# First expert's weights and rows fetched before the recurrence ends, receptance mix moved from the finish phase into the experts

## The chip, the cores and the metric

One core of one Trainium2 chip runs the whole program as one launch. The metric is the time of one execution on the device in microseconds (us), the median of the runs.

## What is computed

The input x has 16 sequences of 512 steps and 512 features; a conditioning vector per sequence goes in as well. Four blocks are chained as residuals:

```python
x = x + _L0_cond_ref(x, cond_1024[:, None, :], ...)   # 16-tap convolution, projections, decayed scan over time
x = x + _L1_cond_ref(x, cond_1024, Wx, Wh, b)          # an LSTM of 512 units over 512 steps
x = x + _L2_cond_ref(x, itok, cond_1024, ...)          # 16 experts, with a receptance gate
x = x + _L3_cond_ref(...)                              # a mask by thresholds along time, as abs(x) >= gathered
```

What the change touches is the third block (the fourth is listed for its place in the code):

```python
xprev = jnp.concatenate([shift_state[:, None, :], x[:, :-1]], axis=1)
dxprev = xprev - x
xk = x + dxprev * time_maa_k
xr = x + dxprev * time_maa_r
...
expert_in = buf[:E * C].reshape(E, C, D)
h = jnp.square(jax.nn.relu(jnp.einsum('ecd,edf->ecf', expert_in, w_key)))
expert_out = jnp.einsum('ecf,efd->ecd', h, w_value)
...
r = jax.nn.sigmoid(jnp.einsum('btd,ed->bte', xr, w_recept))
return r * y
```

Each token has an expert by a hash of its id, and a slot in this expert's buffer of 512 rows. The rows xk are scattered to these slots, the experts run, and their output rows are gathered back, multiplied by the receptance r and added.

## The kernel before

Three functions run one after another, each in a block of its own, with a program for each engine and a barrier of all engines at the end (`recur_phase`, block from line 203; `expert_phase`, from line 932; `finish_phase`, from line 1122). Order within an engine is written out by hand, with semaphores between engines. SP issues the plain loads and stores, POOL (GpSimd) the scatters, gathers and stores of expert outputs; ACT is ScalarE, DVE VectorE and PE TensorE. At the end of a block every engine drains, and the block's line carries these instructions.

`recur_phase` computes the first two blocks in 32 tiles of 16 time steps. PE multiplies the hidden state by Wh (line 415) and, between the steps, the next tile's inputs by Wx in three products of split operands (lines 888 to 890, `split_products`); DVE transposes, adds and makes the cell; ACT does the nonlinear functions. Ahead of the first tile stands a prologue: the 16-tap convolution of tiles 0 and 2 on DVE (`convolve`, lines 644 and 648), of tile 1 on PE with diagonal matrices (`convolve1`, line 372, four filters of 32 instructions), the outputs of the first block (`outputs`, lines 385 and 386), the sum `add_block` (line 701), and the split of its result into a high part on ACT (`split_high`, line 521) and a low part on DVE (`split_low`, line 715). PE's last work before the first step are `inputs(2, q)` (line 363) and `project(2, 0)` (line 351). `load_window` on SP (line 217) waits for a count of `u_part`, which `inputs` raises. Wh is loaded by ACT (line 586) once the four filters are evicted, since it takes the memory of the diagonal matrices; when it has landed, POOL fills the expert rows in memory with zeros (line 316, 16 stores of 1 MB).

For each tile, x2 (the residual after the LSTM) is stored to `x2_scratch` by SP, and twice a tile 128 rows xk are mixed (ACT line 539, DVE line 726), transposed by PE (line 396), copied by ACT (`keep_rows`, line 548) and scattered by POOL (line 309). There is one buffer `rows` and one `index`; both the copy and the index wait until the scatter before has landed. The last two scatters, after the last tile, close the phase.

`expert_phase` runs 16 experts of 512 rows. SP loads rows (line 939), wk (946) and wv (951), 1, 2 and 2 MB. PE transposes the rows of the next expert (973) in the middle of the first product, ACT and DVE split rows, wk and wv into high and low parts (ACT 1015 and 1032, DVE 1051 to 1059 and 1076). The first product takes 8 groups f of 12 matmuls, whose relu and square ACT makes (1027, 1031); the second takes 4 groups a of 24, evicted by ACT (1041) and stored by POOL (960). For expert 0, rows, wk and wv are first loaded after the barrier.

`finish_phase` takes the 16 sequences (batches) in turn. POOL gathers the rows of outputs (1154, four of 256 KB for a batch) and puts the first column of each x2 buffer in place (`halo`, 1159); SP loads x2 (1128). ACT weighs the previous step (`weigh_last`, 1231), DVE mixes it in (`mix_in`, 1297), PE multiplies by w_recept (`receptance`, 1194: 32 instructions for a batch, in two banks by turns), and ACT opens the gate from it (`open_gate`, 1239). PE transposes the gathered rows (`turn`, 1205) and DVE combines gate, rows and x2 (`combine`, 1308 and 1311). Then comes the mask: ACT takes absolutes with a sum (1246), DVE inverts it (`invert`, 1315 and 1319), ACT exponentiates (1254), DVE scans along time (1326), ACT takes the sides of a limit (1263), DVE chooses, searches (1341) and keeps (1350), POOL multiplies (1180) and SP stores (1139). In DVE's loop the order for batch i is:

```python
scan(i)
bound(i)
if i + 1 < B:
    combine(i + 1)
if i + 3 < B:
    mix_in(i + 3)
choose(i)
if i + 1 < B:
    invert(i + 1)
search(i)
keep(i)
```

## Time and profile before

| | us |
|---|---|
| Median of 3 runs (lowest, highest) | 4111.47 (4107.68, 4112.68) |
| The profiled execution | 4110.3 |
| Its span, first to last instruction | 4108.6 |
| PE busy | 3880.3 (94%) |
| DVE busy | 3022.5 (74%) |
| ACT busy | 1696.7 (41%) |
| POOL busy | 290.3 (7%) |

The mean granted clock of PE over the span was 0.985 of full speed. The span has three stages: the recurrence to about 2982 us, the experts from the first product at 3015.4 to the last at 3765.3, and the finish phase, whose first scan starts at 3815.6. Since the phases have different bounds, the shares above say little by themselves; busy times have to be read in windows, and the seams between phases in a timeline. A row of the timeline has the start, the duration, the engine, line and operation, what is written and read, the count, and in brackets how long the engine was idle before it and what ended that.

### The profile page before, as it was taken

To read this page: it belongs to the slowest core of one execution; us is meant where nothing else is said; L and a number is where in the kernel's file an instruction comes from. 1 tells how busy PE (TensorE), PEld (TensorE's weight loads), DVE (VectorE), ACT (ScalarE), POOL (GpSimd) and SP (SyncE) were. 2 spreads that over 40 slices of the span, in tenths; PEclk is the share of its full clock that TensorE was granted. 3 is DMA by queue.
4 is the path that set the end of the run, shared out by engine and by line. 5 is a ranking of instruction groups with operands and counts; after the bars stand their busy time and mean duration, and the time that the engine had idled before them with its cause. 6 is when DMAs were issued, how large, how long until landed. Compare 5 with 4: busy or idle time off the path is not lost. (4 is left out here: it accounts for less than half of the span.)

```text
span 4108.6 us, 111991 instructions
## 1 busy us (share of the span) xinstructions
PE 3880.3 (94%) x44162; PEld 2552.2 (62%) x44162; DVE 3022.5 (74%) x9889; ACT 1696.7 (41%) x5364; POOL 290.3 (7%) x362
## 2 busy tenths in 40 slices
PE   7999999999999999999999999999769999997995
PEld 6566666666656666665666666666457888775442
DVE  7888888888878888887888888875545544552798
ACT  5334333333433333343333333433234444443675
POOL 1000000000000000000000000000000000001343
PEclk9999999999999999999999999999989999998998
DMA  6311111112111111211111112100043343333353
GB/s 241 83 29 27 27 35 27 33 37 30 27 28 35 27 32 30 37 27 28 27 35 27 32 36 31 27 17 15 12 166 123 137 157 135 123 113 123 123 185 113
DMA packets 387868, 266.99 MB, mean 65 GB/s; under 512 B 288953, under 2 KB 322233, under 8 KB 384292
## 3 DMA queue, kind: packets, MB, share of 16 engines
q1 hardware_dynamic: 365648, 184.21, 18.1%
q0 software_dynamic: 17696, 66.79, 4.2%
q10 hardware_dynamic: 4020, 9.10, 0.6%
q8 instruction: 339, 5.55, 0.6%
q14 instruction: 165, 1.35, 0.1%
HBM read 176.48 MB, written 83.92 MB: 63 GB/s over the span
## 5 line engine op out<-in xcount | busy, mean ns | idle before, releaser
L415 PE MATMUL bank<-buf,buf 128*16 128x256 f32 x32768 | 1872.3, 380 | 64.3 <-DVE buf L754 55.0
L415 PEld LDWEIGHTS bank<-buf,buf 128*16 128x16 f32 x32768 | 905.9, 97 | 885.6 <-DVE buf L754 81.8
L888 PE MATMUL bank<-buf,buf 128*128 128x256 f32 (+1 forms) x3072 | 1036.0, 337 | 5.6 <-DVE buf L1059 2.7
L889 PE MATMUL bank<-buf,buf 128*128 128x256 f32 (+1 forms) x3072 | 977.7, 318 | 0.0
L890 PE MATMUL bank<-buf,buf 128*128 128x256 f32 (+1 forms) x3072 | 977.1, 318 | 0.0
L648 DVE SCALAR_TENSOR_TENSOR buf<-buf,buf,buf 128x256 f32<-128x256 f32 x1860 | 846.7, 481 | 0.8 <-issue 0.8
L732 DVE STREAM_TRANSPOSE buf<-bank 128x256 f32<-128x256 f32 x1024 | 459.6, 449 | 447.4 <-PE bank L415 407.8
L604 ACT ACTIVATE buf<-buf 128x96 f32<-128x96 f32 x1024 | 290.6, 284 | 1137.8 <-DVE buf L737 1137.5
L888 PEld LDWEIGHTS bank<-buf,buf 128*128 128x128 f32 x3072 | 580.7, 189 | 255.7 <-issue 216.2
L890 PEld LDWEIGHTS bank<-buf,buf 128*128 128x128 f32 x3072 | 582.8, 190 | 41.1
L889 PEld LDWEIGHTS bank<-buf,buf 128*128 128x128 f32 x3072 | 583.6, 190 | 38.6
L607 ACT ACTIVATE buf<-buf 128x32 f32<-128x32 f32 x1024 | 235.1, 230 | 631.1 <-DVE buf L749 631.1
L1071 DVE CAST buf<-buf 128x512 fp32r<-128x512 f32 x128 | 54.6, 427 | 355.6 <-ACT buf L1031 352.2
L737 DVE SCALAR_TENSOR_TENSOR buf<-buf,buf 128x128 f32<-128x128 f32 x1024 | 295.6, 289 | 21.1 <-DVE buf L732 1.4
L1194 PE MATMUL bank<-buf,buf 128*128 128x512 f32 x512 | 231.4, 607 | 46.6 <-DVE buf L1297 23.7
L309 POOL DMA_INDIRECT expert_in_scratch<-buf,buf x64 | 80.6, 1260 | 2414.1 <-ACT buf L548 2371.2
L527 ACT ACTIVATE buf<-bank,buf 128x256 f32<-128x256 f32 x512 | 233.9, 457 | 15.1 <-PE bank L890 15.1
L754 DVE SCALAR_TENSOR_TENSOR buf<-buf,buf 128x32 f32<-128x32 f32 x1024 | 193.8, 189 | 62.2 <-ACT buf L607 14.2
L749 DVE SCALAR_TENSOR_TENSOR buf<-buf,buf 128x32 f32<-128x32 f32 x1024 | 196.5, 192 | 36.0 <-DVE buf L746 0.7
L605 ACT ACTIVATE buf<-buf 128x32 f32<-128x32 f32 x1024 | 218.6, 213 | 0.0
L1194 PEld LDWEIGHTS bank<-buf,buf 128*128 128x128 f32 x512 | 97.0, 194 | 169.8 <-issue 136.2
L743 DVE SCALAR_TENSOR_TENSOR buf<-buf,buf 128x32 f32<-128x32 f32 x1024 | 176.5, 172 | 17.9 <-ACT buf L604 14.8
(143 smaller groups left out, 2969.2 us busy)
## 6 DMA issues: line engine op xcount, KB each, us to landing
buf<-in_wk SPq DMA_DIRECT2D x16, 2048.0 KB, 9.9
buf<-in_wv SPq DMA_DIRECT2D x16, 2048.0 KB, 9.3
buf<-in_xT SPq DMA_DIRECT2D x62, 496.0 KB, 3.9
buf<-in_xB SPq DMA_DIRECT2D x32, 512.0 KB, 3.8
expert_in_scratch<-buf POOLq DMA_DIRECT2D x16, 1024.0 KB, 22.2
x_scratch<-buf SPq DMA_DIRECT2D x32, 512.0 KB, 9.6
buf<-expert_in_scratch SPq DMA_DIRECT2D x16, 1024.0 KB, 11.9
expert_out_scratch<-buf POOLq DMA_DIRECT2D x64, 256.0 KB, 4.8
```

The source lines that it names most:

```text
L415: last = mm(gate_ps[hf][32 * j:32 * j + B, 0:HCOLS], hist[:, k, at_step(slot_at)], wh[:, k, j * GCOLS + hf * HCOLS:j * GCOLS + (hf + 1) * ...
L527: a(xw[par][:, :, q, :], xw_ps[q % 2][:, 0:LTILE].rearrange("p (b t) -> p t b", b=B), ACT.Identity, bias=bias[:, q:q + 1], scale=0.5).then ...
L604: a(gate[hf], pre[hf][:, 0:6, :], ACT.Tanh, scale=0.5).then_inc(s["ifo_ready"][hf], 1)
L605: a(gcand[hf], pre[hf][:, 6:8, :], ACT.Tanh).then_inc(s["g_ready"][hf], 1)
L607: a(tanh_c[hf], cell[hf], ACT.Tanh, scale=0.5).then_inc(s["tc_ready"][hf], 1)
L648: v.scalar_tensor_tensor(out=conv[:, k, :], in0=src, scalar=taps[:, k, i:i + 1], in1=conv[:, k, :], op0=ALU.mult, op1=ALU.add).then_inc(s[ ...
L732: v.transpose(turned_g[hf].rearrange("p g b -> p (g b)"), gate_ps[hf][:, 0:HCOLS])\
L737: v.scalar_tensor_tensor(out=pre[hf], in0=turned_g[hf][:, :, 0:B], scalar=0.5, in1=xw[par][:, st, 8 * hf:8 * hf + 8, :], op0=ALU.mult, op1 ...
L888: nc.tensor.matmul(out, left[0], right[0], start=first, stop=False)
L889: nc.tensor.matmul(out, left[0], right[1], start=False, stop=False)
L890: return nc.tensor.matmul(out, left[1], right[0], start=False, stop=last)
L1194: last = nc.tensor.matmul(r_ps[m % 2][:, 0:T], wr[:, k, m * P:(m + 1) * P], xr[i % 2][:, k, :], start=k == 0, stop=k == KD - 1)
```

## The change

It has six parts.

1. In the prologue the order changes on three engines. PE runs `project(0, 1)` and `inputs(0, 1)` ahead of the third filter, and the fourth filter behind `outputs(0, ...)` and `inputs(1, ...)`. ACT evicts the first two filters, splits x1, then evicts the other two and loads Wh. DVE runs `convolve(2, 1, ...)` ahead of `split_low(1, 1, ...)`.
2. SP loads wk and wv of expert 0 in the recurrence's last tile, into memory that the recurrence no longer uses; ACT and DVE split wk at the end of their programs of the recurrence.
3. The last scatter has a row buffer of its own and takes its index straight from `slot`; so neither the copy nor the scatter waits for the scatter before.
4. SP loads the rows of expert 0 in the recurrence's block, when all scatters have landed.
5. Weighing and mixing for the receptance leave the finish phase. In each expert e, SP loads x2 of batch e with its first column (`load_x2`, the column as a copy from a small buffer `halo` in fast memory), ACT weighs one of four parts after each eviction of y, DVE mixes the parts after the split of the next wk, and SP stores the result to a new scratch `xr_scratch`, once the mix is complete. This wait, store and load stand in SP's program ahead of the loads of the next expert's wk.
6. The finish phase loads the mixed rows (`load_mixed`, three buffers). w_recept, the first three mixed rows and x2 of batches 0 and 1 are loaded during the last expert, and PE and ACT run the receptance and gate of batches 0 and 1 at the end of the experts' block.

```diff
--- before.py
+++ after.py
@@ -111,6 +116,7 @@
     window = carve(KD, WIN)
     center = carve(KD, LTILE)
     conv = carve(KD, LTILE)
+    rows_last = carve(D, at=carve.top)
     x1_hi, x1_lo = ([carve(KD, LTILE, dt=F32R) for _ in range(2)] for _ in range(2))
...
@@ -255,10 +261,17 @@
                     load_window(n + 4, 1)
 
             tiles(sp, tile)
+            sp.wait_ge(s["xw_summed"], NBLK * NLT)
+            first.load_wk(sp, ins, 0)
+            sp.wait_ge(s["pre_ready"][0], LSTEPS * (NLT - 1))
+            sp.wait_ge(s["pre_ready"][1], LSTEPS * (NLT - 1))
+            first.load_wv(sp, ins, 0)
             sp.wait_ge(s["x2_done"], 2 * NLT)
             sp.dma_start(x2_d.rearrange("p c b t -> p (c b) t")[:, :, (NLT - 1) * LSTEPS:],
                          stream[3].rearrange("p c b t -> p (c b) t")[:, :, 1:])\
                 .then_inc(s["x2_stored"][1], 16)
+            sp.wait_ge(s["scattered"], 16 * 2 * NLT)
+            first.load_rows(sp, rows_d, 0, 0)
             for par in range(2):
                 sp.wait_ge(s["x2_stored"][par], 16 * NLT // 2)
...
@@ -318,6 +331,14 @@
             pool.dma_start(y_d[E * CAP:E * CAP + 1, :], zeros[0:1, 0:D]).then_inc(s["zero_stored"], 16)
             g.tensor_scalar(stream[0][:, :, :, 0], cond, 2.0, None, ALU.mult).then_inc(s["halo_ready"], 1)
 
+            def scatter_last():
+                r = 2 * NLT - 1
+                pool.wait_ge(s["rows_ready"], r + 1)
+                pool.sem_inc(s["pool_passed"], 1)
+                g.indirect_dma_start(out=rows_d, out_offset=bass.IndirectOffsetOnAxis(ap=slot[:, r:r + 1], axis=0),
+                                     in_=rows_last, in_offset=None, bounds_check=E * CAP - 1,
+                                     oob_is_err=False).then_inc(s["scattered"], 16)
+
             def tile(n, pair, four, ahead):
                 if later(n, 1):
...
@@ -331,8 +352,8 @@
                         scatter(n - 1, u)
 
             tiles(pool, tile)
-            for u in range(2):
-                scatter(NLT - 1, u)
+            scatter(NLT - 1, 0)
+            scatter_last()
             pool.wait_ge(s["scattered"], 16 * 2 * NLT)
 
         @block.tensor
...
@@ -428,15 +449,15 @@
             project(0, 0)
             inputs(0, 0)
             convolve1(1)
-            convolve1(2)
             project(0, 1)
             inputs(0, 1)
-            convolve1(3)
+            convolve1(2)
             pe.wait_ge(s["steps"], 7)
             for q in range(2):
                 outputs(0, q)
             for q in range(2):
                 inputs(1, q)
+            convolve1(3)
             for q in range(2):
                 project(1, q)
...
@@ -543,6 +564,9 @@
             def keep_rows(m, u):
                 r = 2 * m + u
                 act.wait_ge(s["rows_turned"], r + 1)
+                if isinstance(r, int) and r == 2 * NLT - 1:
+                    a(rows_last, rows_ps[:, :], ACT.Copy).then_inc(s["rows_ready"], 1)
+                    return
                 if later(m, 1) or u:
                     act.wait_ge(s["scattered"], 16 * r)
...
@@ -580,12 +604,17 @@
             soft_last(0)
             state_high(0)
             act.wait_ge(s["proj_part"], 2)
-            for k in range(KD):
+            def keep_conv1(k):
                 act.wait_ge(s["conv1_summed"], k // 2 * 2 + 2)
                 a(conv[:, k, :], conv_ps[k], ACT.Identity, bias=conv_b[:, k:k + 1]).then_inc(s["conv1_ready"], 1)
-            act.dma_start(wh, ins["Wh"]).then_inc(s["wh_landed"], 16)
+
+            for k in range(2):
+                keep_conv1(k)
             for q in range(2):
                 split_high(0, 0, q)
+            for k in range(2, KD):
+                keep_conv1(k)
+            act.dma_start(wh, ins["Wh"]).then_inc(s["wh_landed"], 16)
             soft_first(1)
             soft_last(1)
...
@@ -624,6 +653,7 @@
             for u in range(2):
                 weigh_last(NLT - 1, 3, u)
                 keep_rows(NLT - 1, u)
+            first.high_wk(act, 0)
 
         @block.vector
...
@@ -840,9 +870,9 @@
                 state_part(1, i)
             for q in range(2):
                 add_block(1, 0, 1, q)
+            convolve(2, 1, 0, CONVS // 2)
             for q in range(2):
                 split_low(1, 1, q)
-            convolve(2, 1, 0, CONVS // 2)
 
             def tile(n, pair, four, ahead):
...
@@ -880,6 +910,7 @@
             tiles(dve, tile)
             for u in range(2):
                 mix_in(NLT - 1, 3, u)
+            first.low_wk(dve, 0)
 
 
...
+        sp.dma_start(self.wk_raw, ins["wk"][:, bass.ds(e * KD, KD), :]).then_inc(self.s["wk_landed"], 16)
+
+    def load_wv(self, sp, ins, e):
+
+        sp.dma_start(self.wv_raw, ins["wv"][:, bass.ds(e * KF, KF), :]).then_inc(self.s["wv_landed"], 16)
+
+    def load_rows(self, sp, rows_d, e, par):
+
+        src = rows_d[bass.ds(e * CAP, CAP), :].rearrange("(a p) d -> p a d", p=P)
+        sp.dma_start(self.rows[par], src).then_inc(self.landed[par], 16)
+
+    def high_wk(self, act, e):
+
+        act.wait_ge(self.s["wk_landed"], 16 * (e + 1))
+        for k in range(KD):
+            self.nc.scalar.activation(self.wk_hi[:, k, :], self.wk_raw[:, k, :], ACT.Copy)\
+                .then_inc(self.s["wk_hi_ready"], 1)
...
+class Gating:
+
+    RING, XR_RING = 6, 3
+
+    def __init__(self, nc, ctx, carve, banks):
+        self.nc = nc
+        self.stream = [carve(KD, T) for _ in range(self.RING)]
+        self.gate = [carve(KD, T) for _ in range(2)]
+        self.wr = carve(KD, D)
+        self.xr = [carve(KD, T) for _ in range(self.XR_RING)]
...
+    def load_mixed(self, sp, xr_d, i):
+
+        if i >= self.XR_RING:
+            sp.wait_ge(self.s["r_summed"], KD * (i - self.XR_RING + 1))
+        sp.dma_start(self.xr[i % self.XR_RING], xr_d[:, :, i, :]).then_inc(self.xr_landed[i % self.XR_RING], 16)
+
+    def receptance(self, pe, i):
+
+        pe.wait_ge(self.xr_landed[i % self.XR_RING], 16 * (i // self.XR_RING + 1))
+        for m in range(KD):
+            if i >= 1 or m >= 2:
+                pe.wait_ge(self.s["gate_ready"], KD * i + m - 1)
+            for k in range(KD):
+                last = self.nc.tensor.matmul(self.r_ps[m % 2][:, 0:T], self.wr[:, k, m * P:(m + 1) * P],
+                                             self.xr[i % self.XR_RING][:, k, :], start=k == 0, stop=k == KD - 1)
+            last.then_inc(self.s["r_summed"], 1)
...
-                    sp.wait_ge(s["wk_ready"], KD * e)
-                sp.dma_start(wk_raw, ins["wk"][:, bass.ds(e * KD, KD), :]).then_inc(s["wk_landed"], 16)
+                    sp.wait_ge(first.s["wk_ready"], KD * e)
+                    first.load_wk(sp, ins, e)
                 if not is_last(e):
                     load_rows(e + 1, 1 - par)
                 if later(e, 1):
                     sp.wait_ge(s["wv_ready"], KF * e)
-                sp.dma_start(wv_raw, ins["wv"][:, bass.ds(e * KF, KF), :]).then_inc(s["wv_landed"], 16)
+                    first.load_wv(sp, ins, e)
+                if later(e, 1):
+                    sp.wait_ge(s["xr_made"], KD * e)
+                    store_mixed(e - 1)
+                else:
+                    sp.dma_start(maa_r, ins["maa_r"]).then_inc(s["maa_landed"], 16)
+                    sp.wait_ge(s["halo_made"], 1)
+                load_x2(e)
 
             experts(sp, one)
+            sp.wait_ge(s["turned"], KD * E)
+            sp.wait_ge(first.s["wk_ready"], KD * E)
+            sp.wait_ge(s["xr_stored"], 16 * (E - 1))
+            sp.dma_start(gating.wr, ins["wr"]).then_inc(gating.s["wr_landed"], 16)
+            for i in range(gating.XR_RING):
+                gating.load_mixed(sp, xr_d, i)
+            sp.wait_ge(s["h_summed"], KF * E)
+            for i in range(2):
+                gating.load(sp, x2_d, i)
+            sp.wait_ge(s["xr_made"], KD * E)
+            store_mixed(E - 1)
+            sp.wait_ge(s["xr_stored"], 16 * E)
 
         @block.gpsimd
         def _(pool):
...
 
             experts(pe, one)
+            pe.wait_ge(s["xT_ready"], KD * E)
+            pe.wait_ge(gating.s["wr_landed"], 16)
+            for i in range(2):
+                gating.receptance(pe, i)
 
...
-                act.wait_ge(s["wk_landed"], 16 * (e + 1))
-                if later(e, 1):
-                    act.wait_ge(s["h_summed"], KF * e)
-                for k in range(KD):
-                    nc.scalar.activation(wk_hi[:, k, :], wk_raw[:, k, :], ACT.Copy).then_inc(s["wk_hi_ready"], 1)
-
-            split_wk(0)
+                act.wait_ge(s["h_summed"], KF * e)
+                first.high_wk(act, e)
+
+            def weigh_last(e, k):
+                if k == 0:
+                    if not later(e, 1):
+                        act.wait_ge(s["share_ready"], 2)
+                    act.wait_ge(s["x2_landed"], 32 * (e + 1))
+                    if later(e, 1):
+                        act.wait_ge(s["xr_stored"], 16 * e)
+                nc.scalar.activation(xr_row[:, k, :], x2_row[:, k, 0:T], ACT.Copy, scale=maa_last[:, k:k + 1])\
+                    .then_inc(s["weighed"], 1)
 
             def one(e, par):
-                act.wait_ge(s["wv_landed"], 16 * (e + 1))
+                act.wait_ge(first.s["wv_landed"], 16 * (e + 1))
                 if later(e, 1):
                     act.wait_ge(s["y_summed"], NS * e)
...
@@ -1039,8 +1201,11 @@
                     elif a >= 2:
                         act.wait_ge(stored[a % 2], 16 * (a // 2))
                     nc.scalar.activation(y[a % 2], y_ps[a % 2][:, :], ACT.Copy).then_inc(s["y_ready"], 1)
+                    weigh_last(e, a)
 
             experts(act, one)
+            for i in range(2):
+                gating.open_gate(act, i, 0, KD)
 
         @block.vector
...
                     if f > TURN_FROM and f <= TURN_FROM + KD and not is_last(e):
                         split_x(e + 1, 1 - par, f - TURN_FROM - 1)
                 if not is_last(e):
-                    split_wk(e + 1)
+                    first.low_wk(dve, e + 1)
+                for k in range(KD):
+                    mix_in(e, k)
 
...
+                gating.load(sp, x2_d, i)
+                if i + 1 < RING:
+                    gating.load_mixed(sp, xr_d, i + 1)
             for i in range(B):
-                sp.wait_ge(s["final_ready"], i + 1)
+                sp.wait_ge(final_ready, i + 1)
                 sp.dma_start(out.rearrange("p (k b t) -> p k b t", k=KD, b=B)[:, :, i, :], final).then_inc(stored, 16)
                 if i + RING < B:
-                    load(i + RING)
+                    gating.load(sp, x2_d, i + RING)
+                    gating.load_mixed(sp, xr_d, i + RING)
             sp.wait_ge(stored, 16 * B)
 
...
-                        pe.wait_ge(s["gated_ready"], KD * (i - 1) + k + 1)
+                        pe.wait_ge(gated_ready, KD * (i - 1) + k + 1)
                     for c in range(NC):
                         last = nc.tensor.transpose(t_ps[k][:, c * P:(c + 1) * P],
                                                    rows[i % 2][c][:, k * P:(k + 1) * P], ident)
                     last.then_inc(s["turned"], 1)
 
-            pe.wait_ge(s["weights_landed"], 16)
-            receptance(0)
             turn(0)
-            receptance(1)
             turn(1)
-            receptance(2)
+            gating.receptance(pe, 2)
             for i in range(B):
                 if i + 2 < B:
                     turn(i + 2)
...
```

## Rows read from the trace of the kernel before

**Rows 1.** Windows by stage: busy us (and count) by engine, granted clock, DMA share, GB/s.

```profile
3015.44:3765.25 749.81, 730.42 (x3312) 599.19 (x3312) 369.16 (x567) 318.81 (x509) 34.08 (x63) 1.00 0.35 128
3765.25:3815.55 50.30, 25.33 (x65) 11.69 (x64) 14.09 (x26) 14.13 (x28) 14.46 (x23) 0.76 0.59 212
3848.38:4086.52 238.14, 202.60 (x620) 99.12 (x618) 233.83 (x441) 172.81 (x436) 107.68 (x72) 0.97 0.45 159
```

**Rows 2.** Timelines of PE and of DVE in the prologue.

```profile
51.09 7.17 PE L372 MATMUL bank<-buf,buf 128*128 128x256 f32 x32
97.79 3.65 PE L415 MATMUL bank<-buf,buf 128*16 128x256 f32 x64
...
95.99 1.29 DVE L715 TENSOR_TENSOR buf<-buf,buf 128x512 fp32r<-128x512 f32 x2 [12.37 <-ACT buf L521]
97.85 11.96 DVE L648 SCALAR_TENSOR_TENSOR buf<-buf,buf,buf 128x256 f32<-128x256 f32 x30
```

**Rows 3.** Line 217, its load issued at 96.0: time from issue to landing.

```profile
DMA to landing us min/median/max: 11.1/11.1/11.1
```

**Rows 4.** Timeline of all engines at the end of the recurrence.

```profile
2987.03 1.09 PE L396 MATMUL bank<-buf,buf 128*128 128x128 f32 x4 [2.37 <-DVE buf L726]
2990.85 0.60 ACT L548 ACTIVATE buf<-bank 128x512 f32<-128x512 f32 x1 [4.36 <-DMA expert_in_scratch<-buf,buf]
...
2992.31 0.97 POOL L309 DMA_INDIRECT expert_in_scratch<-buf,buf  x1 [1.20 <-ACT buf L548]
```

**Rows 5.** Line 203, the recurrence's block: duration (ns) and start of POOL's drain.

```profile
L203 POOLq DRAIN  x1: 6692/6692/6692, 2995.3 to 2995.3; - x1
```

**Rows 6.** Timeline of PE and DVE at the first expert's start.

```profile
3007.58 1.97 PE L973 MATMUL bank<-buf,buf 128*128 128x128 f32 x8 [19.46 <-DMA buf<-expert_in_scratch]
...
3013.47 0.69 DVE L1053 TENSOR_TENSOR buf<-bank,buf 128x512 fp32r<-128x512 f32 x1
...
3015.44 0.77 PE L888 MATMUL bank<-buf,buf 128*128 128x512 f32 x1 [2.73 <-DVE buf L1059]
```

**Rows 7.** Timeline of ACT in expert 1: its first relu, its split of wk.

```profile
3067.52 0.60 ACT L1027 ACTIVATE buf<-bank 128x512 f32<-128x512 f32 x1 [2.26 <-PE bank L890]
...
3091.59 3.90 ACT L1015 ACTIVATE buf<-buf 128x1024 fp32r<-128x1024 f32 x4
```

**Rows 8.** Line 946, the 16 loads of wk: time from issue to landing.

```profile
DMA to landing us min/median/max: 9.1/9.9/10.5
```

**Rows 9.** Line 932, the experts' block: duration (ns) and start of POOL's drain.

```profile
L932 POOLq DRAIN  x1: 5279/5279/5279, 3768.9 to 3768.9; - x1
```

**Rows 10.** Timelines of POOL, PE and DVE at the start of the finish phase.

```profile
3779.04 0.95 POOL L1154 DMA_INDIRECT buf<-expert_out_scratch,buf  x1 [0.30 <-issue]
...
3789.15 16.56 PE L1194 MATMUL bank<-buf,buf 128*128 128x512 f32 x32 [23.75 <-DVE buf L1297]
...
3806.26 0.69 DVE L1308 SCALAR_TENSOR_TENSOR buf<-buf,bank 128x512 f32<-128x512 f32 x1 [10.63 <-PE bank L1205]
```

**Rows 11.** Line 1154, the 64 gathers: time from issue to landing.

```profile
DMA to landing us min/median/max: 3.7/6.9/8.2
```

**Rows 12.** Timelines of DVE and PE in the finish phase's periods.

```profile
3962.02 2.73 DVE L1297 SCALAR_TENSOR_TENSOR buf<-buf,buf,buf 128x512 f32<-128x512 f32 x4
...
4051.52 1.91 PE L1205 MATMUL bank<-buf,buf 128*128 128x128 f32 x16
4053.27 13.90 PE L1194 MATMUL bank<-buf,buf 128*128 128x512 f32 x32
4067.00 1.91 PE L1205 MATMUL bank<-buf,buf 128*128 128x128 f32 x16
...
4071.10 4.55 DVE L1326 TENSOR_TENSOR_SCAN buf<-buf,bank 128x512 f32<-128x512 f32 x4
4081.97 0.17 DVE L1315 TENSOR_SCALAR buf<-buf 128x4 f32<-128x4 f32 x1 [0.71 <-ACT buf L1246]
4086.52 4.55 DVE L1326 TENSOR_TENSOR_SCAN buf<-buf,bank 128x512 f32<-128x512 f32 x4
```

208 lines of the change are left out of this document (93 added, 115 removed).

## The prediction

> **What bounds the kernel now.** I read the busy table by stages first, then at each seam between stages the timeline of all engines, then the instructions of single lines. Three phases follow one another, each an instruction block with a barrier at its end. The recurrence (to about 2982 us) is a chain of small steps that the change doesn't touch. The experts are TensorE work: PE is busy 730.4 of 749.8 us [rows 1], so work added on ScalarE (ACT) or VectorE (DVE) there is free while it fits its gaps. In the finish phase DVE is busy 233.8 of 238.1 us from the second scan to the sixteenth, PE 202.6 [rows 1]: DVE bounds it. Between the last expert product (3765.25) and the second scan (3848.38) lie 83.1 us, with a granted clock of 0.76 up to the first scan (3815.55) [rows 1]: a fill whose chain is serial. The change works on the fill at three seams and on the finish period. Times below are those of the profile before, and a gain at an early seam is not carried into the times of a later one.
>
> **Prologue.** Before, DVE waited 12.37 us for ACT's split of x1 (L521) at 95.99, and only then did the 32 operations of the second half convolution, which end at 109.8; PE had begun the first recurrent products at 97.79 and was done by 101.4 [rows 2]. With the convolution ahead of the split, DVE runs it in that wait: from 83.6 for some 12.6 us, then the split, at about 97.9. What is late next is PE. Its fourth filter (7.17 us [rows 2]) now stands behind the outputs and inputs, so that the load of Wh issues some 6 us later, and the products I work out 0.6 us later; TensorE's first step would come at about 101 instead of 109.7, a gain of 8.5. But in this step DVE convolves with a window whose load PE's inputs release; it took 11.1 us from its issue at 96.0 [rows 3] and would land at 107.7, when that convolution could have begun at 103. It began at 111.9, 2.1 after the transpose; I take 111.9 - 107.7 = 4.2. Bounds: 8.5 if the window is early, -1 if the filter and the later Wh load cost more and the landing takes 16 us beside the zero stores, which shift too.
>
> **From the recurrence to the first expert's products.** Before, the last rows' copy on ACT waited 4.36 us for the scatter ahead of it, and began at 2990.85 though PE's transposes were done at 2988.1 [rows 4]. With a buffer of its own it runs at 2988.15 to 2988.75; GpSimd (POOL) needed 0.86 us from the copy's end to the scatter [rows 4], so the scatter issues at 2989.6 in place of 2992.31. Before, POOL's drain began 3.0 after the issue and took 6.69 us, to 3002.0, which opened the next block [rows 5]. The first scatter may now overlap, so I allow 0.2: the barrier opens at 2999.5, 2.5 earlier (the bounds are 0, if the drain waits for the same last packet, and 3). The rows' load is released by the scatters, about 2992.5, and is there by 2998; weights come in the last tile, whose ACT and DVE waits are long. So PE transposes at 2999.8 instead of 3007.58 (it had waited 19.46 for the rows), DVE's split of x needs 6.58 (3007.58 to 3014.16), and the first product, which waited 2.73 more for the weights' split, starts at 3006.4 instead of 3015.44 [rows 6]. ACT's and DVE's splits of wk (four each, 3.9 us on ACT [rows 7]) lie under the drain, ended by 2995. Gain 9.0. Bounds: 6 with a later drain, 11 if the clock comes back sooner.
>
> **Experts.** Added to each: four ACTIVATEs, four DVE operations of 2.73 us together (those of L1297 [rows 12]), a 1 MB load, a 1 MB store and a load of 512 single elements. ACT's last one stands between the last eviction and the next expert's relu, where ACT sat idle 2.26 us [rows 7]; it needs 0.62. DVE's then ends before the relu is squared. On SP's queue the new wait for the mixed row stands ahead of the next wk load, and moves it from 3052 to about 3068.5. It is needed at 3091.59 [rows 7], and such a load takes 9.1 to 10.5 us [rows 8]; with 2 MB ahead of it I allow 16, against 23. The next rows' load, behind it, has an expert's length to spare. Cost 0; bounds 0 and +0.5 per expert, 8 in all, for a queue that I can't see.
>
> **The seam to the finish phase.** Before: the drain of POOL ended at 3774.2 [rows 9], eight gathers were issued with the fourth at 3779.04, the halo operations stood behind them, the first receptance ran 3789.15 to 3805.7 (16.56 us for 32 instructions, which take 13.90 at full clock [rows 10, 12]), and DVE's first combine began at 3806.26 [rows 10]. Now receptances 0 and 1 follow the last expert product without a barrier, still at full clock: 3765.25 + 2 x 13.75 = 3792.8. Their inputs were loaded from 3731 on. The barrier now waits for PE and ACT, not for the drain: 3793.6, 19.4 later than before. The fourth gather issues 4.84 after it, at 3798.4, and lands 6.9 later (median of 64, range 3.7 to 8.2 [rows 11]): 3805.3. The transposes, on a cold PE, let combine begin at 3806.5, so nothing is won up to there. Without the mixing behind it the chain from combine to scan is 1.86 shorter (next part): the first scan is at 3813.9 instead of 3815.55 [rows 1], gain 1.6, bounds -1 and +5. From there before took 32.8 us to the second scan [rows 1], since receptance 1 and 2 stood before its combine. Now combine 1 runs at once; receptance 2 starts about 3812.2 cold, its second quarter ends near 3821.6 (a quarter is 3.4 us, and I add 2.7 for the cold clock, as 16.56 against 13.90), then nine ACTIVATEs of 512 columns (gate, four sides, four absolutes), about 0.65 each by the 0.60 of [rows 7] and so 5.9 as an estimate, and DVE's rest of 4.55 (4081.97 to 4086.52 [rows 12]): second scan at 3832.2, 18.3 after the first. Gain 14.5, bounds 12 and 17.
>
> **The finish period.** DVE loses 2.73 us of mixing per batch [rows 12], but not all comes back. At the end, where no batch is left to mix, the scans start 15.42 apart (4071.10, 4086.52), and DVE waits 0.71 us for ACT's last absolute [rows 12]: mixing had covered that. Before, 12 periods lasted (238.14 - 2 x 15.42) / 12 = 17.27 [rows 1]. PE is next: transposes and receptance start 1.75 apart, the receptance takes 13.90 with 0.16 of it under its neighbour [rows 12], together 15.49. I take PE's 15.49. Coupling: ACT opens two gates at once after its exponents; with the mixing's ACTIVATEs gone it does so 2.5 us earlier, and I estimate a slack of about 1 us for PE's phase against DVE's in which neither side waits (gate 0 is out some 3.7 after a scan's start, and gate 1 may be out as late as 5.4 before ACT's sides delay the absolutes). Twelve periods of 17.27 become 15.49 and the last two stay within 0.1: 21.3. Bounds: 8 if each handshake costs 1.1 us more, 22.
>
> **Sum.** 4.2 + 9.0 + 0 + 1.6 + 14.5 + 21.3 = 50.6. The profiled execution took 4110.3 (span 4108.6, 1.7 around it), 1.2 less than the median of 4111.47. Forecast: 4110.3 - 50.6 = 4059.7, say 4060. Its own range is 4052 to 4068.
>
> **Rivals.** *Handshakes on PE.* When PE and DVE both need 15.4 to 15.5 us, waits for gates add up instead of hiding. For it: PE waited for ACT's gate in each period before. Against it: the gate follows earlier. With 1.1 us in each of 13 periods, 4074. Chance 0.14.
>
> *Gathers late.* SP queues five loads of 1 MB at the moment of the first gathers. If the gathers shared so badly that they took twice their median, 13.8 us, combine would begin 6.9 later, and the time is 4067. Against it: none of 64 gathers took over 8.2 [rows 11], beside loads that were issued with them. Chance 0.06. The Trainium skill, DMA: Bandwidth & Descriptors, "Issuing engines are not separate DMA queues", says that DMAs of all issuing engines run on the same 16 engines and interleave. By that rule POOL's gathers do share with SP's loads, which speaks for this rival; the landings bear out a sharing, not a place at the end.
>
> *The early parts don't bite.* If the drain ends when it did and the window's load holds the prologue, the two seams give 6.5 rather than 13.2, and the time is 4067, at the rim of my range; with one more shortfall, 4072. Chance 0.06.
>
> *More than forecast.* The window lands early and the gathers in 4 us: 4060 - 4 - 4 = 4052, down to 4047. Chance 0.06.
>
> *Slower than before.* The wk load of the next expert, held behind the wait for the mixed row, lands after ACT needs it; ACT's queue then holds the evictions of y behind it, and PE stalls. It decides from a landing of 23 us, and from 27 (3.6 us x 14 experts = 50) the kernel is slower. At 30 us: 4060 + 7 x 14 = 4158. Landings of 9.1 to 10.5 [rows 8] speak against it. Chance 0.02, and 0.02 for a landing near 26, which would eat the gain: 4060 + 3 x 14 = 4102.
>
> **How the numbers follow.** Forecast within its own range 0.64; the rest above. The range for 8 in 10 takes in the forecast's range and most of the cases next to it: 4050 to 4076. A measurement can tell about 0.2%, 8 us. Faster by more: 0.96; within it: 0.02 (the landing near 26); slower by more: 0.02.
>
> **What would show it.** First recurrent transpose near 101, the convolution behind it near 108; first expert product 9 us earlier; 47.0 us per expert as before; receptances straight behind the last product at 13.75 each; scans 15.5 apart, with PE almost gapless. Wrong would be: ACT waiting for wk, PE stalls behind the evictions, scans 16.5 or more apart, a combine that starts after 3812.

## The result, and the profile after

The changed kernel takes 4068.86 us (median of 4 runs, 4065.98 to 4069.88) against 4111.86 for the kernel before (4107.68 to 4112.68): a ratio of 0.9896, 95% interval 0.9879 to 0.9913. That is 43.0 us less where 50.6 were forecast, and 8.9 us over the forecast of 4060. The profiled execution took 4065.98 us with a span of 4064.0, which is 44.6 less than the span before.

Windows by stage of the changed kernel, from the first expert product to the last eviction of y, from there to the first scan, and from the second scan to the sixteenth; columns as in [rows 1], whose windows have the same cuts but for 3765.25, which lies 0.19 ahead of the last eviction (3765.44):

```profile
3001.55:3760.66 759.11, 739.75 (x3313) 600.53 (x3314) 412.00 (x629) 357.58 (x571) 34.13 (x63) 1.00 0.49 175
3760.66:3809.00 48.34, 35.05 (x102) 17.86 (x101) 6.54 (x12) 9.79 (x21) 12.79 (x17) 0.86 0.47 173
3824.50:4041.57 217.07, 199.22 (x620) 100.05 (x618) 203.86 (x393) 146.19 (x388) 110.05 (x62) 0.96 0.65 229
```

The first row is the surprise. The experts take 9 us longer than before, and PE is busy 9.3 us longer (739.75 against 730.42, 0.2 of it already the first receptance) on the same products at the same granted clock. The third row is the forecast gain of the finish. By stage, as differences of the same events in the two traces:

| stretch | before | after | forecast gain | measured gain |
|---|---|---|---|---|
| start to the last but one copy of rows (prologue) | 2984.70 | 2980.19 | 4.2 | 4.5 |
| from there to the first expert product | 30.74 | 21.36 | 9.0 | 9.4 |
| first product to last eviction of y (experts) | 750.00 | 759.11 | 0 | -9.1 |
| last eviction to first scan | 50.11 | 48.34 | 1.6 | 1.8 |
| first to second scan | 32.83 | 15.50 | 14.5 | 17.3 |
| second to sixteenth scan | 238.14 | 217.07 | 21.3 | 21.1 |
| sixteenth scan to the end | 22.1 | 22.4 | 0 | -0.3 |
| sum | | | 50.6 | 44.6 |

**Prologue.** DVE's timeline, which answers to [rows 2] and [rows 3]:

```profile
83.54 11.96 DVE L678 SCALAR_TENSOR_TENSOR buf<-buf,buf,buf 128x256 f32<-128x256 f32 x30
95.43 1.27 DVE L745 TENSOR_TENSOR buf<-buf,buf 128x512 fp32r<-128x512 f32 x2
99.29 0.45 DVE L762 STREAM_TRANSPOSE buf<-bank 128x256 f32<-128x256 f32 x1 [2.58 <-PE bank L436]
...
106.68 0.41 DVE L674 TENSOR_SCALAR buf<-buf,buf,buf 128x256 f32<-128x256 f32 x1 [5.17 <-DMA buf<-in_xT]
```

The convolution fills the old wait, the first transpose comes 10.4 us earlier, and then DVE waits 5.17 us for the window's load, as the forecast said it would (it expected 101 and 108; the rows say 99.3 and 106.7).

**To the first product.** Timeline of ACT, POOL and PE at the end of the recurrence, and the row of POOL's drain (line 209), which answer to [rows 4 to 6]:

```profile
2983.64 0.60 ACT L568 ACTIVATE buf<-bank 128x512 f32<-128x512 f32 x1 [1.65 <-PE bank L417]
...
2985.11 0.98 POOL L338 DMA_INDIRECT expert_in_scratch<-buf,buf  x1 [2.48 <-ACT buf L568]
...
2994.95 1.94 PE L1126 MATMUL bank<-buf,buf 128*128 128x128 f32 x8 [11.35 <-PEq L209]
...
3001.55 0.79 PE L919 MATMUL bank<-buf,buf 128*128 128x512 f32 x1 [1.51 <-DVE buf L1218]
```

```profile
L209 POOLq DRAIN  x1: 6692/6692/6692, 2988.0 to 2988.0; - x1
```

The last copy no longer waits for the scatter ahead of it. The drain has the same 6692 ns, and PE now waits for the block (L209) and not for the rows. PE's transposes and DVE's split of x are what is left between the barrier and the first product.

**Seam to the finish.** Timeline of PE, POOL and DVE; it answers to [rows 10, 12]:

```profile
3760.46 27.63 PE L1006 MATMUL bank<-buf,buf 128*128 128x512 f32 x64
...
3793.63 0.94 POOL L1309 DMA_INDIRECT buf<-expert_out_scratch,buf  x1 [0.30 <-issue]
...
3800.20 3.64 PE L1340 MATMUL bank<-buf,buf 128*128 128x128 f32 x16 [12.11 <-DMA buf<-expert_out_scratch,buf]
3801.43 0.69 DVE L1409 SCALAR_TENSOR_TENSOR buf<-buf,bank 128x512 f32<-128x512 f32 x1 [12.20 <-PE bank L1340]
...
3805.02 1.94 PE L1340 MATMUL bank<-buf,buf 128*128 128x128 f32 x16 [1.18 <-DMA buf<-expert_out_scratch,buf]
3806.80 13.90 PE L1006 MATMUL bank<-buf,buf 128*128 128x512 f32 x32
```

Two receptances take 27.63 us straight behind the last product, and PE then waits 12.11 us for the gathers. From line 1309, the 64 gathers, the answer to [rows 11]:

```profile
DMA to landing us min/median/max: 3.7/6.8/8.6
```

These are all 64 gathers of the phase. At the seam itself five loads of SP's queue, 1 MB each, were issued from 3788.99 on, and the fourth gather, issued at 3793.63, had landed when the transposes began at 3800.20: at most 6.6 us. So the gathers landed as before.

### The profile page after: what moved, and what is told of

Same layout as the page of the kernel before. It is cut to its first block and busy times, and to the rows that moved or that the text cites. A ratio compares the mean times of both kernels' runs of the same rounds, so it can differ in the third digit from the quotient of the medians.

```text
span 4064.0 us, 112079 instructions
## 1 busy us (share of the span) xinstructions
PE 3882.5 (96%) x44162; PEld 2553.4 (63%) x44162; DVE 3026.2 (74%) x9889; ACT 1700.8 (42%) x5364; POOL 302.9 (7%) x346
## 5 line engine op out<-in xcount | busy, mean ns | idle before, releaser
L919 PEld LDWEIGHTS bank<-buf,buf 128*128 128x128 f32 x3072 | 581.1, 189 | 254.8 <-issue 210.9
L921 PEld LDWEIGHTS bank<-buf,buf 128*128 128x128 f32 x3072 | 583.4, 190 | 44.1
L920 PEld LDWEIGHTS bank<-buf,buf 128*128 128x128 f32 x3072 | 584.2, 190 | 41.2
L767 DVE SCALAR_TENSOR_TENSOR buf<-buf,buf 128x128 f32<-128x128 f32 x1024 | 294.7, 288 | 21.1 <-DVE buf L762 1.4
L784 DVE SCALAR_TENSOR_TENSOR buf<-buf,buf 128x32 f32<-128x32 f32 x1024 | 193.4, 189 | 62.6 <-ACT buf L636 14.2
L779 DVE SCALAR_TENSOR_TENSOR buf<-buf,buf 128x32 f32<-128x32 f32 x1024 | 196.3, 192 | 35.9 <-DVE buf L776 0.6
L1006 PE MATMUL bank<-buf,buf 128*128 128x512 f32 x512 | 222.2, 592 | 0.0
L1223 DVE SCALAR_TENSOR_TENSOR buf<-buf,buf,buf 128x512 f32<-128x512 f32 x64 | 48.0, 750 | 205.4 <-ACT buf L1178 205.4
L773 DVE SCALAR_TENSOR_TENSOR buf<-buf,buf 128x32 f32<-128x32 f32 x1024 | 175.7, 172 | 17.8 <-ACT buf L633 14.7
L776 DVE SCALAR_TENSOR_TENSOR buf<-buf,buf 128x32 f32<-128x32 f32 x1024 | 188.3, 184 | 0.0
## 6 DMA issues: line engine op xcount, KB each, us to landing
buf<-in_wk SPq DMA_DIRECT2D x16, 2048.0 KB, 10.7
```

Of the source, the lines that this page charges most:

```text
L767: v.scalar_tensor_tensor(out=pre[hf], in0=turned_g[hf][:, :, 0:B], scalar=0.5, in1=xw[par][:, st, 8 * hf:8 * hf + 8, :], op0=ALU.mult, op1 ...
L919: nc.tensor.matmul(out, left[0], right[0], start=first, stop=False)
L920: nc.tensor.matmul(out, left[0], right[1], start=False, stop=False)
L921: return nc.tensor.matmul(out, left[1], right[0], start=False, stop=last)
L1006: last = self.nc.tensor.matmul(self.r_ps[m % 2][:, 0:T], self.wr[:, k, m * P:(m + 1) * P], self.xr[i % self.XR_RING][:, k, :], start=k == ...
```

## Why the experts became slower

PE's waits in the experts are the same in both traces: 19.4 us, 15 times, all before the third transposes of an expert, for DVE's split of x. So nothing new waits. The products themselves come at another pace. Timeline of PE in the second projection of expert 1, changed kernel:

```profile
3085.97 0.40 PE L919 MATMUL bank<-buf,buf 128*128 128x512 f32 x1
3086.21 0.40 PE L920 MATMUL bank<-buf,buf 128*128 128x512 f32 x1
3086.44 0.39 PE L921 MATMUL bank<-buf,buf 128*128 128x512 f32 x1
3086.67 0.39 PE L919 MATMUL bank<-buf,buf 128*128 128x512 f32 x1
3086.91 0.39 PE L920 MATMUL bank<-buf,buf 128*128 128x512 f32 x1
```

The same in the kernel before:

```profile
3099.23 0.39 PE L888 MATMUL bank<-buf,buf 128*128 128x512 f32 x1
3099.45 0.39 PE L889 MATMUL bank<-buf,buf 128*128 128x512 f32 x1
3099.68 0.39 PE L890 MATMUL bank<-buf,buf 128*128 128x512 f32 x1
3099.91 0.39 PE L888 MATMUL bank<-buf,buf 128*128 128x512 f32 x1
```

The starts lie 232.5 ns apart (mean of 72); before they lie 226.8 apart (mean of 74), and in the first projection of both kernels 226.7. An expert has 96 products in its second projection: 96 x 16 x 5.7 ns = 8.8 us of the missing 9.1. Two things had changed for them: the mixing's traffic and operations ran beside them, and the buffers of the mixing, carved in front of them, had moved the hidden tiles (hid_hi and hid_lo, the stationary operands) by 16,768 bytes, which is an odd multiple of 128. The four kernels of the first group tell the two apart.

**1. Mixing's buffers behind y** (rows_behind):

```diff
-    x2_row, xr_row = carve(KD, 1 + T), carve(KD, T)
-    halo, maa_r, maa_last, maa_now = carve(KD, B), carve(KD), carve(KD), carve(KD)
     relu = [carve(CAP) for _ in range(2)]
...
     y = [carve(D) for _ in range(2)]
+    x2_row, xr_row = carve(KD, 1 + T), carve(KD, T)
+    halo, maa_r, maa_last, maa_now = carve(KD, B), carve(KD), carve(KD), carve(KD)
```

> The changed kernel, with the mixing's buffers (x2 row, mixed row, halo, coefficients) placed behind the hidden tiles and y instead of in front of them, so that relu, square, hid_hi, hid_lo and y lie at the addresses of the kernel before. Nothing else differs. Theory A (addresses): in the changed kernel each of the 96 products of an expert's second projection issues 232 ns after the one before, against 226.7 ns in the kernel before, only because hid_hi and hid_lo, the stationary operands, moved by 16,768 bytes to 1664 over a multiple of 2048, where all other operands lie at 1280. It expects 226.7 ns, 46.9 us per expert, and 4057 to 4061 us in all, 8.5 to 9 below the changed kernel. Rival B (traffic): the mixing's transfers and operations slow TensorE's reads; it expects 232 ns and no change, 4066 to 4069.

Measured: 4059.6 us (median of 4), 0.9878 of before (0.9861 to 0.9894), with products 226.8 ns apart. The window from the first product to the last eviction of this kernel, to hold against the first row above:

```profile
3003.06:3752.73 749.67, 730.24 (x3313) 599.30 (x3314) 412.08 (x629) 355.88 (x570) 34.15 (x63) 1.00 0.51 177
```

The 9.4 us are back with all the traffic still there (DMA share 0.51, DVE 412 us busy). Theory A stands, rival B falls.

**2 and 3. A gap of 128 bytes, and one of 1664,** in front of hid_hi (gap128, gap1664; the latter has carve(416), and carve counts words of 4 bytes):

```diff
+    carve(32)
     hid_hi, hid_lo = carve(KF, CAP, dt=F32R), carve(KF, CAP, dt=F32R)
```

> The changed kernel with a gap of 128 bytes behind the mixing's buffers: relu, square and the hidden tiles start at a multiple of 256 bytes again (1792 over a multiple of 2048), as in the kernel before, but not at the place within 2048 that the other operands have. Theory A1 (the start's place within 256 bytes counts): 226.7 ns per product, about 4058. Theory A2 (the place within 2048 relative to the other operands counts): 232 ns, about 4067. Rival B (traffic): 232 ns, about 4067.

> The changed kernel with a gap of 1664 bytes behind the mixing's buffers: the hidden tiles are at 1280 over a multiple of 2048 again, as all other operands, but 18,432 bytes higher than in the kernel before. Theories A1 and A2: 226.7 ns per product, about 4058. Theory A3 (it is the region high in the memory that is slow, hid_lo lying above 190,000 bytes): 232 ns, about 4067. Rival B (traffic): 232 ns, about 4067.

Measured: both 226.7 ns, 4058.64 and 4058.24 us in one run each. In gap128 the hidden tiles start at a multiple of 256 bytes (counted from the start of the memory that the kernel carves up) and at another place within 2048 than the other operands; in gap1664 they lie higher than in any other kernel. So neither the place within 2048 nor the region counts; A1, the place within 256 bytes, is left. (The gap stands in front of hid_hi only, so relu and square kept their odd place, against what my expectation said of them; they are no operands of PE, and it did no harm.)

**4. The kernel before with a gap of 16,768 bytes** (before_gap; no mixing):

```diff
+    carve(4192)
     hid_hi, hid_lo = carve(KF, CAP, dt=F32R), carve(KF, CAP, dt=F32R)
```

> The kernel before, with an unused gap of 16,768 bytes in front of the hidden tiles, so that they lie at the addresses of the changed kernel; no mixing, nothing else changed. Theory A (addresses, of any kind): the second projection's products slow from 226.7 to 232 ns, and the kernel takes 8.5 to 9 us more, about 4120.5. Rival B (traffic): no change, 4111.

Measured: 4119.96 us (8 runs), 1.0024 of before (1.0013 to 1.0034). The same window, where [rows 1] has 749.81 and 730.42:

```profile
3014.91:3773.98 759.07, 739.64 (x3312) 599.95 (x3312) 369.29 (x567) 320.13 (x510) 34.25 (x63) 1.00 0.35 127
```

An unused gap alone makes the loss, in a kernel without any mixing. PE's weight loads stay as long (599.95 us busy, 599.19 before); it is the distance of the products that grows. The Trainium skill, SBUF — State Buffer, "Who interferes with whom", says that DMAs never contend with a compute engine for that memory and that PE waits on no other engine. The trace agrees: with the mixing's traffic and operations beside them (rows_behind) the products start 226.8 ns apart, as without.

**5. The moving operand 128 bytes off** (wv_gap; the edit as it stands against rows_behind, which has the mixing's buffers behind y):

```diff
+    carve(32)
     wv_hi, wv_lo = carve(KF, D, dt=F32R), carve(KF, D, dt=F32R)
+    carve(32)
```

> The changed kernel with the mixing's buffers behind y, and with 128 unused bytes in front of and behind wv_hi and wv_lo: now the moving operands of the second projection start 128 bytes over a multiple of 256, the stationary ones (hid_hi, hid_lo) at a multiple. Theory A1s (only the stationary operand's place counts): 226.7 ns per product, about 4058. Rival A1m (any operand's place counts): 232 ns, about 4067.

Measured: 233.3 ns, 4068.78 us in one run, 9.2 above rows_behind. PE's timeline in the second projection of expert 1:

```profile
3085.56 0.40 PE L919 MATMUL bank<-buf,buf 128*128 128x512 f32 x1
3085.80 0.39 PE L920 MATMUL bank<-buf,buf 128*128 128x512 f32 x1
3086.03 0.40 PE L921 MATMUL bank<-buf,buf 128*128 128x512 f32 x1
3086.27 0.39 PE L919 MATMUL bank<-buf,buf 128*128 128x512 f32 x1
```

A1s falls: a moving operand off by 128 bytes costs about the same as a stationary one. Both off together was not tried, so it stays open whether each operand's own place counts or whether the two must agree; nor was any shift other than 0 and 128 over a multiple of 256.

## What each part of the change is worth

Each kernel here is the changed kernel with one part undone, in one run. Absolute times of one run mix in where the recurrence happens to end (its last but one copy lay between 2976.5 and 2981.7 in eleven kernels with the new prologue), so I read differences from the nearest event.

**6. DVE's order in the prologue** (split_ahead):

```diff
-            convolve(2, 1, 0, CONVS // 2)
             for q in range(2):
                 split_low(1, 1, q)
+            convolve(2, 1, 0, CONVS // 2)
```

> The changed kernel with VectorE's order in the prologue as before: the split of x1 stands ahead of the second half convolution again; the orders of TensorE and ScalarE stay changed. Theory: the prologue's gain, 4.5 us as the recurrence's last tile shows it, comes from this order alone, and all later marks move 4 to 5 us later (4069.5 profiled in place of 4066.0). Rival: the landing of the next window sets the step from which the recurrence runs freely, and the marks move by under 1.5 us.

Measured: 4069.39 us. The last but one copy comes at 2982.93, 3.0 later than the mean of the eleven (2979.9), where 4 to 5 were expected; the kernels with the old prologue have it at 2984.70 (before) and 2983.93 (before_gap). With that spread these marks can't tell 3 us from 4.5. The marks in the prologue itself are closer. DVE in split_ahead:

```profile
108.21 0.44 DVE L762 STREAM_TRANSPOSE buf<-bank 128x256 f32<-128x256 f32 x1
...
110.34 0.41 DVE L674 TENSOR_SCALAR buf<-buf,buf,buf 128x256 f32<-128x256 f32 x1
```

In before_gap, which has the old prologue whole, the same two stand at 108.22 and 110.36, and `add_block` begins at 81.54 (81.53 here). So without DVE's order the new orders of PE and ACT win nothing at these marks. With it (106.68 in the changed kernel, `add_block` at 81.69) the second mark comes 24.7 to 25.7 us after the start of `add_block` in the eleven kernels, against 28.8: 3.1 to 4.1 us. The profile of the kernel before has the second mark at 111.86, 1.5 later than before_gap with the same prologue, so some of the 4.5 us is spread between executions.

**7. Rows loaded behind the barrier** (rows_barrier):

```diff
-            first.load_rows(sp, rows_d, 0, 0)
...
+                if not later(e, 1):
+                    first.load_rows(sp, rows_d, 0, 0)
```

> The changed kernel with the first expert's rows loaded at the start of the experts' block, behind the barrier, as before; weights still early. Theory: the load, issued some 0.4 us after the barrier (about 2995.5) and 5.3 us in landing, lets TensorE's transposes begin at about 3001 in place of 2994.95: the first product comes 6 us later, 3007.5. The time is 6 us more, about 4072. Rival: the queue's drain and the weights' split set the start anyway; under 2 us later.

Measured: 4071.77 us. Its timeline of ACT, SP and PE:

```profile
2979.95 0.60 ACT L567 ACTIVATE buf<-bank 128x512 f32<-128x512 f32 x1 [1.65 <-PE bank L416]
...
2991.23 0.92 SPq L951 DMA_DIRECT2D buf<-expert_in_scratch  x2
...
2996.80 1.97 PE L1127 MATMUL bank<-buf,buf 128*128 128x128 f32 x8 [16.89 <-DMA buf<-expert_in_scratch]
...
3003.44 0.79 PE L918 MATMUL bank<-buf,buf 128*128 128x512 f32 x1 [1.51 <-DVE buf L1219]
```

From the last copy to the first product it takes 23.49 us against 17.91 (2983.64 to 3001.55): 5.6 later, for 6 expected. (The second scan follows the first after 18.8 us here, with transposes 1 at half clock; that is taken up in the account of the prediction.)

**8. Last scatter from the shared buffer** (one_buffer):

```diff
-                if isinstance(r, int) and r == 2 * NLT - 1:
-                    a(rows_last, rows_ps[:, :], ACT.Copy).then_inc(s["rows_ready"], 1)
-                    return
...
-            scatter_last()
+            scatter(NLT - 1, 1)
```

> The changed kernel with the last scatter from the shared buffer again, waiting for the scatter ahead of it. Theory: the last scatter issues 2.5 to 3 us later (its copy waits for the landing of the one ahead), and the drain, the barrier, the rows' load and the first product come 2.5 to 3 us later. Rival: the drain of the queue ends with the same last packet, and the first product moves by under 1 us.

Measured: 4069.78 us; from the last but one copy (2980.34) to the first product (3004.40) 24.06 us against 21.36: 2.7, as expected. Of the 9.4 us of this seam 2.7 are the buffer and 5.6 the rows' load. The 1.1 us that are left would be the weights' early load and split; that part was not undone by itself.

**9. Receptances 0 and 1 back in the finish phase** (receptance_behind):

```diff
             experts(pe, one)
-            pe.wait_ge(s["xT_ready"], KD * E)
-            pe.wait_ge(gating.s["wr_landed"], 16)
-            for i in range(2):
-                gating.receptance(pe, i)
...
+            pe.wait_ge(gating.s["wr_landed"], 16)
+            gating.receptance(pe, 0)
             turn(0)
+            gating.receptance(pe, 1)
             turn(1)
...
```

> The changed kernel with receptances 0 and 1 and their gates back in the finish phase, in the order of the kernel before (receptance 0, transposes 0, receptance 1, transposes 1, receptance 2); mixing stays in the experts. Theory C (the mixing's move carries the gain, the receptances' place does not): the barrier then opens at about 3770, the gathers land by 3782, receptance 0 on a cold engine ends near 3788, the first scan comes 6 to 14 us earlier than 3809.0, and the second within 2 us of 3824.5; time within 2 us of the changed kernel. Rival D (the receptances behind the last product carry it, as my forecast put it): the second scan comes 12 us or more later, time 4078.

Measured: 4064.93 us. Its timeline of PE:

```profile
3768.18 15.53 PE L1006 MATMUL bank<-buf,buf 128*128 128x512 f32 x32 [9.14 <-PEq L1058]
3783.55 1.91 PE L1334 MATMUL bank<-buf,buf 128*128 128x128 f32 x16
3785.30 7.03 PE L1006 MATMUL bank<-buf,buf 128*128 128x512 f32 x16
3795.60 8.63 PE L1006 MATMUL bank<-buf,buf 128*128 128x512 f32 x16 [3.27 <-ACT buf L1016]
3804.06 1.91 PE L1334 MATMUL bank<-buf,buf 128*128 128x128 f32 x16
```

The barrier opens early, the first scan comes at 3791.88, 17 us earlier, and the second at 3823.33. Counted from the last eviction of y (3759.07) the second scan comes after 64.3 us, against 63.8 in the changed kernel and 82.9 before. So of the 19.1 us that the change wins up to the second scan, the receptances' new place gives 0.4 in this pair of traces and what is left of the change gives 18.7; that this is above all the mixing done in the experts is argued, not shown by an edit of its own. Even the sign of the 0.4 is not sure: the changed kernel's 63.8 is a case of full clock at transposes 1, and in four other kernels whose code here is the same those ran at half clock and the second scan came 66.0 to 67.1 us after the eviction. PE idles 9.14 us ahead of the barrier here and 12.11 us behind it there: the same hole in two places. My forecast gave the two stretches 16.1 us together and put them down to the wrong edit.

**10 and 11. What bounds the finish period** (invert_later; light_receptance, which has invert later too and leaves out a quarter of the receptance's sum from batch 3 on):

```diff
                 choose(i)
+                search(i, 0, 2)
                 if i + 1 < B:
                     invert(i + 1)
-                search(i)
+                search(i, 2, KD)
```

```diff
+            ks = KD if i < 3 else KD - 1
-            for k in range(KD):
+            for k in range(ks):
...
```

> The changed kernel with VectorE's invert of the next batch behind the first two searches of this one, so that ScalarE's last absolute is hidden; same work. The finish period is 15.505 us on VectorE (14.79 of its own and 0.71 of waiting), and 15.482 on TensorE. Theory E (two bounds within 0.02 us of each other): the 0.71 us wait goes, TensorE takes over at 15.48, and the fourteen periods give back 0.3 us. Rival F (only VectorE's handshake bounds): 14.8 per period, 9.8 us in all, 4056 profiled.

> As the run before, with VectorE's invert later, and the receptances from the fourth batch on sum three of four 128-row parts of their input: that part of the computation is left out, a quarter of TensorE's receptance (3.4 us per batch). Theory E: with TensorE at about 12.1 us the period falls to VectorE's own 14.8, in all 9 us less than the changed kernel. Rival G (something else, such as ScalarE's gates or the loads, holds the period at 15.5): no change.

Measured: 4062.65 and 4056.14 us. From the second to the sixteenth scan 215.54 and 207.54 us, against 217.07; from the first to the second 14.82 in both, against 15.50. So with invert later the scans start 14.8 apart twice and then meet PE at 15.48: 2.2 us gained in all where E had 0.3 and F 9.8. With PE lightened as well every period is 14.82. The two bounds of the changed kernel's period (15.49, and 15.48 with PE alone as the bound) lie within about 0.02 us of each other. Taking away DVE's alone was worth 2.2 of some 10 us; PE's alone was not taken away.

## A faster version

Four edits on the changed kernel (combined): the mixing's buffers behind y, invert later, DVE's split of the next x moved to the head of an iteration, and TensorE half a receptance ahead in the finish. The third one, on the wait of 19.4 us:

```diff
                 for f in range(KF):
+                    if f > TURN_FROM and f <= TURN_FROM + KD and not is_last(e):
+                        split_x(e + 1, 1 - par, f - TURN_FROM - 1)
                     dve.wait_ge(s["square_ready"], KF * e + f + 1)
...
-                    if f > TURN_FROM and f <= TURN_FROM + KD and not is_last(e):
-                        split_x(e + 1, 1 - par, f - TURN_FROM - 1)
```

and the fourth:

```diff
+                if i + 3 < B:
+                    gating.receptance(pe, i + 3, 0, 2)
                 if i + 2 < B:
                     turn(i + 2)
                 if i + 3 < B:
-                    gating.receptance(pe, i + 3)
+                    gating.receptance(pe, i + 3, 2, KD)
```

> The changed kernel with four edits: the mixing's buffers behind y (addresses of before); in an expert VectorE splits the next expert's x as the first work of an iteration instead of the last; VectorE's invert behind two searches; and in the finish phase TensorE runs half a receptance ahead (the first two quarters of receptance i+3 before the transposes of i+2, those of batch 2 before transposes 0, ScalarE's gates in step). Same work. By the runs before it: addresses 8.7 us; the wait of 1.3 us before the third transposes of an expert, 19.4 us over 15 experts, goes, since VectorE was idle for 1.44 us just where the split can now stand; the finish period falls from 15.5 to 14.8 for as long as TensorE's head start of 6.9 us lasts, 14 periods at 0.68 less some 3 us, 6 to 9 us in all. Sum 34 to 37 us under the changed kernel's 4068.9: 4032 to 4035. Rival H (the wait in the experts is ScalarE's or the rows' landing, at most 3 us of it goes): 4050. Rival I (the half receptance ahead stalls behind the gates): 4040.

Measured: 4034.68 us (median of 5), 0.9813 of before (0.98 to 0.9826). Its window from first product to last eviction, and PE's timeline in the finish:

```profile
3002.23:3729.76 727.53, 727.53 (x3313) 601.89 (x3314) 412.10 (x629) 355.95 (x571) 34.15 (x63) 1.00 0.52 182
```

```profile
3777.79 13.90 PE L1006 MATMUL bank<-buf,buf 128*128 128x512 f32 x32
3791.53 1.91 PE L1340 MATMUL bank<-buf,buf 128*128 128x128 f32 x16
3793.28 13.90 PE L1006 MATMUL bank<-buf,buf 128*128 128x512 f32 x32
3807.01 1.91 PE L1340 MATMUL bank<-buf,buf 128*128 128x128 f32 x16
```

The experts are now all PE: 727.53 of 727.53 us, 22.1 less than in rows_behind (19.4 expected): the 19.4 us of waiting are gone, and PE's busy time fell by 2.7 as well, which no run explains. But the half receptance ahead gave nothing: PE still repeats every 15.48 us, the scans too, and from the last eviction to the end it takes 302.9 us, where invert_later alone takes 301.4. ACT waits 2.7 us for PE's quarter before it may start its sides, and DVE then waits 0.6 for the absolutes behind them; it looks as if the head start only moved which quarter ACT waits for. That is rival I's result but not quite its mechanism, since PE itself doesn't wait in these periods. The total came out in range for two reasons that are not the forecast's: the experts gave 2.7 more, and the sum was taken from the changed kernel's median. Between the two traces the gain is 31.3 us (4064.0 to 4032.7), under the 34 to 37 forecast; the changed kernel's profiled execution was 2.9 under its median.

## Why the prediction was right, and where it was off

The measured 4068.86 us lies in 4050 to 4076, the range for 8 in 10, but 0.9 above the forecast's own range of 4052 to 4068. No rival came true. What moved the time was a cost that no rival named, partly hidden by a gain that was larger than its term: without the latter's 2.8 us the sum would have been off by 8.8 and not by 6.0.

- **Prologue, 4.2: right** (4.5), and for its reason: the window's load ends the wait. By the marks under split_ahead 3.1 to 4.1 is what the order gives, and some of the 4.5 is spread.
- **To the first product, 9.0: right** (9.4). Barrier 2.5 earlier: 2.8. Then 6.9 to the product: 6.9.
- **Experts, 0: wrong, -9.1.** The step that failed is the count of costs: it went through instructions, queues and landings, and found them free, rightly (wk's landings had a median of 10.7 and at most 13.5 us, the split of wk began at 3078.10 without a wait, PE waited no more than before). It left out where the new buffers lie. Its bound of 8 us "for a queue that I can't see" was near the 9.1 by chance, and still under it. With the addresses put right the kernel takes 4059.6, for 4060 forecast.
- **Seam to the first scan, 1.6: right** (1.8). The rival of late gathers didn't come (landings 3.7 to 8.6 us). The Trainium skill, DMA: Bandwidth & Descriptors, "Issuing engines are not separate DMA queues", has all issuers interleave on the same 16 engines. No row here shows which engine carried what; the landings are compatible with a sharing that costs the gathers little, their median going from 6.9 to 6.8 and their longest from 8.2 to 8.6.
- **Second scan, 14.5: mis-sized, 17.3, and for the wrong reason.** I had put it down to receptances 0 and 1 standing behind the last product. receptance_behind undoes just that, and the second scan comes 64.3 us after the last eviction against 63.8. The first scan's term and this one are one chain there: the first comes 17 us earlier and the second 31.5 after it. As for the size, I had receptance 2 start on a slow clock at about 3812.2, and so the scan 18.3 us after the first. In the profiled execution it started at 3806.80 at full clock, and the distance was 15.5. Which of the two happens goes with the clock at transposes 1. Windows over the transposes 0 and 1 in the changed kernel, and over transposes 1 in rows_behind:

```profile
3800.10:3804.90 4.80, 3.64 (x16) 3.27 (x16) 3.36 (x6) 1.42 (x4) 0.86 (x5) 0.59 1.03 383
3804.90:3806.80 1.90, 1.78 (x16) 1.81 (x17) 1.87 (x3) 0.75 (x3) 1.60 (x2) 1.00 1.05 388
```

```profile
3797.20:3800.70 3.50, 3.41 (x16) 3.44 (x17) 2.22 (x5) 1.77 (x6) 2.61 (x3) 0.50 1.05 387
```

With a granted clock of 0.50 (1.2 GHz) the sixteen transposes take 3.65 us and the second scan follows after 17.6 to 17.7 (rows_behind, gap1664, wv_gap) or 18.8 (rows_barrier, where the receptance behind them took 15.1 us and not 13.9); with 1.00 (2.4 GHz) they take 1.94, and it follows after 15.5 to 15.6 (the changed kernel, gap128, one_buffer, split_ahead). Code that is the same at this place gets either; with one trace of each kernel it stays open whether that goes by kernel or by execution. My 18.3 was a forecast of the slow case.
- **Finish, 21.3: right** (21.1), period 15.50 for 15.49 forecast. That PE sets it was half the truth: DVE's chain with ACT's last absolute sets nearly the same value (runs 10 and 11).
- **What would have shown it wrong:** none of the stalls that I listed came. The loss showed in another place of that list, the 47.0 us per expert that I had asked for: the trace gives 47.4 (759.11 / 16), with no wait to explain it.

## What to carry to other kernels

A new buffer is not free because it fits: it moves all that is carved after it, and here one matmul operand that ended up 128 bytes off a multiple of 256 slowed every product by 2.5 to 3%. Carve additions behind the operands of TensorE, and when PE's busy time grows with the same products at the same clock, look at the distance of their starts before looking for a wait. Before taking credit for one edit, put it back alone: the receptances' move looked like the source of 16 us and was worth 0.4, less than the 2.1 us and more that the clock moves at that place.

## What the runs showed of the hardware

- Products of 128x128 by 128x512 in fp32r started 226.7 ns apart with both operands at multiples of 256 bytes (counted from the start of the memory that the kernel carves up), 232.5 with the stationary one 128 bytes off, and 233.3 with the moving one 128 bytes off. The weight loads' own duration (188 to 189 ns) did not change.
- After PE idled for 12.0 to 12.3 us at the seam, transposes 0 took 3.5 to 3.7 us, at a granted clock of 0.50 to 0.55, in all ten kernels with this seam; transposes 1 ran at half clock in four of them (3.65 us) and at full clock in six (1.94).
- POOL's drain at the end of the recurrence took 6692 ns in every kernel, whether the last scatter waited for the one ahead (before, one_buffer) or not.
